# Gated cross-attention and mixture-of-experts blocks: queries turned on the TensorE between two groups of scores, one place sooner

## The reference, cut to what matters

```python
# x: (4, 512, 512) tokens; ctx_512: (4, 512, 128), keys and values at once
def _L0_xattn_ref(q, k, v):              # _L1_xattn_ref computes the same
    QH, KVH = (32, 8); D = E // QH       # D = 16
    G = QH // KVH                        # 4 query heads share a head of keys
    qh = q.reshape(b, s, KVH, G, D).transpose(0, 2, 3, 1, 4)
    kh = k.reshape(b, s, KVH, D).transpose(0, 2, 1, 3)
    vh = v.reshape(b, s, KVH, D).transpose(0, 2, 1, 3)
    scores = jnp.einsum('bkgsd,bktd->bkgst', qh, kh) * scale
    attn = jax.nn.softmax(scores, axis=-1) / DROPOUT
    out = jnp.einsum('bkgst,bktd->bkgsd', attn, vh)
    return out.transpose(0, 3, 1, 2, 4).reshape(b, s, E)

x = x + jnp.tanh(g_xattn[0]) * _L0_xattn_ref(_layernorm(x, axis=-1), ctx_512, ctx_512)
x = x + jnp.tanh(g_ffn[0]) * _L0_ffn_ref(_layernorm(x, axis=-1), ...)   # 8 experts, top 2, and a shared one
x = x + jnp.tanh(g_xattn[1]) * _L1_xattn_ref(_layernorm(x, axis=-1), ctx_512, ctx_512)
x = x + jnp.tanh(g_ffn[1]) * _L1_ffn_ref(_layernorm(x, axis=-1), ...)   # 32 experts, top 6, and a shared one
```

## Time and profile before

| | |
|---|---|
| time, median of 3 runs | 2155.77 us (2149.66 to 2156.09) |
| profiled execution | 2151.34 us, its span 2149.6 us |
| PE busy | 1973.5 us (92%) |
| DVE busy | 1325.7 us (62%) |
| ACT busy | 1105.8 us (51%) |
| POOL busy | 752.2 us (35%) |
| line 597, the takes of the maxima (DVE) | x1024, 644.8 us |
| line 491, the exps (ACT) | x512, 494.0 us |
| line 386, the products for the maxima (PE) | x1024, 407.6 us |
| line 403, the scores for the exps (PE) | x1024, 326.7 us |
| line 418, the products with values (PE) | x2048, 274.5 us |

### The profile page before, as it was taken

How to read it: one execution, slowest core, us unless ns; L and a number is a source line. 1 busy time by engine, 2 the same in 40 slices (tenths; PEclk the granted TensorE clock), 3 DMA queues, 4 the chain that set the end, 5 groups by cost and what they waited for, 6 DMA issues and landing times. The chain is left out here.

```text
span 2149.6 us, 40775 instructions
## 1 busy us (share of the span) xinstructions
PE 1973.5 (92%) x10072; PEld 1222.5 (57%) x10073; DVE 1325.7 (62%) x2547; ACT 1105.8 (51%) x1801; POOL 752.2 (35%) x912
## 2 busy tenths in 40 slices
PE   5999999979999999993999999988789999999997
PEld 2444444334667658882434444433557888888886
DVE  7888888732234325533888888856776455555553
ACT  2777777832112115541577777763113566666664
POOL 3122222112201005554122222221664555565564
PEclk9999999989999999996799999999999999999998
DMA  5322222150000128765422222213005888888886
GB/s 162 88 60 63 56 64 62 29 217 19 1 0 1 69 83 197 169 111 123 132 70 56 56 60 66 56 49 107 0 5 174 190 187 198 200 204 205 202 196 103
DMA packets 96018, 219.90 MB, mean 102 GB/s; under 512 B 16930, under 2 KB 20004, under 8 KB 95908
## 3 DMA queue, kind: packets, MB, share of 16 engines
q1 hardware_dynamic: 61540, 138.80, 22.3%
q0 software_dynamic: 33792, 79.71, 19.1%
q10 hardware_dynamic: 576, 0.00, 0.0%
HBM read 114.64 MB, written 56.63 MB: 80 GB/s over the span
## 5 line engine op out<-in xcount | busy, mean ns | idle before, releaser
L597 DVE TENSOR_REDUCE maxima<-ring_ps 128x1 f32<-128x512 f32 x1024 | 644.8, 681 | 116.2 <-PE ring_ps L386 115.9
L491 ACT ACTIVATE probs<-score_ps 128x1024 f32<-128x1024 f32 x512 | 494.0, 1020 | 47.7 <-PE score_ps L403 45.3
L386 PE MATMUL ring_ps<-k_turned,q_turned 64*128 64x512 f32 x1024 | 407.6, 477 | 32.1 <-DMA q_turned<-q_lo 13.3
L1091 PE MATMUL bank_f<-w_gu_parts_f,xg_T_f 128*128 x1800 | 368.1, 353 | 2.0 <-issue 2.0
L386 PEld LDWEIGHTS ring_ps<-k_turned,q_turned 64*128 64x128 f32 x1024 | 176.9, 192 | 326.1 <-DVE maxima L597 205.8
L1091 PEld LDWEIGHTS bank_f<-w_gu_parts_f,xg_T_f 128*128 128x128 f32 x1800 | 326.6, 190 | 30.2 <-issue 2.6
L403 PE MATMUL score_ps<-q_turned,k_turned 64*128 64x512 f32 x1024 | 326.7, 450 | 14.7 <-ACT probs L491 14.3
L418 PE MATMUL out_ps<-probs,v_ones 128*32 128x512 f32 x2048 | 274.5, 608 | 0.8 <-ACT probs L491 0.7
L1116 PE MATMUL bank_f<-w_dn_parts_f,hg_T_f 96*128 (+1 forms) x888 | 242.6, 409 | 2.5 <-DVE hg_T_f L1653 1.4
L916 POOL DMA_INDIRECT out_x<-y_tok_f,idx_out_f x111 | 176.7, 1592 | 137.4 <-ACT y_tok_f L1291 104.9
L900 POOL DMA_INDIRECT xg_f<-xh_rows_f,idx_in_f x156 | 158.1, 1014 | 186.3 <-DVE idx_in_f L1543 114.5
(11 more groups left out here) (211 smaller groups left out, 2252.2 us busy)
## 6 DMA issues: line engine op xcount, KB each, us to landing
w_gu_f<-in_L_w_gu SPq DMA_DIRECT2D x64, 384.0 KB
q_turned<-q_hi SPq DMA_DIRECT2D x128, 128.0 KB, 2.6
w_dn_f<-in_L_w_dn SPq DMA_DIRECT2D x32, 384.0 KB
k_turned<-k_hi SPq DMA_DIRECT2D x128, 64.0 KB, 2.1
q_turned<-no_max SPq DMA_DIRECT2D x64, 128.0 KB, 2.6
q_turned<-q_lo SPq DMA_DIRECT2D x64, 128.0 KB, 2.6
xh_rows_f<-xh_f SPq DMA_DIRECT2D x8, 1024.0 KB, 9.0
w_gu_f<-in_L_w_gu SPq DMA_DIRECT2D x16, 512.0 KB
```

The costliest lines, as they stand in the source:

```text
L386: pe.matmul(ring(k, "max", i), q_turned[rows, slot, h // 2, c * P:(c + 1) * P], k_turned[rows, slot, :], start=True, stop=True).then_inc(m ...
L491: act.activation(probs[:, c % 2, pair, :, :], score_ps[:, pair, :, :], ACT.Exp, scale=float(D) ** -0.5).then_inc(exped, 1)
L597: dve.tensor_reduce(maxima[:, par, col:col + 1], ring(k, "max", i), AX.X, ALU.max).then_inc(max_taken, 1)
L1091: mm = pe.matmul(bank[:, half, 0:2 * F], xg_T[:, half, x_part, d, :], w_gu_parts[:, bass.ds(par, 1), w_part, d, :].rearrange("p a f -> p ( ...
```

## The change

Two numbers change: `TURN_Q_AT` from 5 to 4, and `COPY_Q_AT` from 6 to 5.

```diff
-TURN_AT, TURN_Q_AT, INVERT_AT = 2, 5, 8
-COPY_OUT_AT, COPY_TURN_AT, COPY_Q_AT = 1, 3, 6
+TURN_AT, TURN_Q_AT, INVERT_AT = 2, 4, 8
+COPY_OUT_AT, COPY_TURN_AT, COPY_Q_AT = 1, 3, 5
```

## The result

| | before | after |
|---|---|---|
| median of 13 runs | 2154.42 us (2149.66 to 2160.61) | 2148.47 us (2143.82 to 2152.71) |
| ratio | | 0.9975, 95% interval 0.9965 to 0.9986 |
| ordinary odd step (k = 5 of batches 0 to 2 apart) | 12.72 us | 12.27 us |
| step k = 5, batches 0 to 2 | 12.86 us | 12.42 us |
| even step | 11.57 us | 11.57 us |

The time lies in the range and 3 us from the number forecast; the gain is 5.4 us by the ratio (its interval is 3.0 to 7.5 us) where 7.9 were forecast. The profiled execution of after is by chance the slowest of its 13 runs (2152.71 us), so spans of single executions say nothing here; steps do.

The account below looks back on a forecast made before the run. Short waits between TensorE and the two engines reading its PSUM set the step. 20 x 0.42 - 4 x 0.13 = 7.9 us off 2151.34 gives 2143.4, plus 2 for level: 2145.5 us; range 2136 to 2154.

Parts of the forecast that it names:

- ordinary odd step: Odd attention steps apart from first steps and k = 3: 20 turns, each step ending 0.42 us sooner.
- The split of the 1.15 us: Extra time of an odd step over an even one: 0.58 us of transposes, 0.56 us of waiting for ScalarE.
- the wait for take 9: Product 11 in the odd step now waits for VectorE's take 9, losing 0.38 us of TensorE.
- The rival in which the ring does not bite: Product 11 finds its bank free: 0.8 us gained per turn, 21 us in all, about 2132; chance 0.11.
- the one in which GpSimd holds up VectorE: Queries' cast and subtraction slow takes 10 to 13: 0.87 us lost per turn, 23 us, about 2176; chance 0.05.
- The rival in which the wait only changes its name: The ring's wait takes all that ScalarE gives back; time within 2 us of now, 2152; chance 0.14.
- steps k = 3: Odd steps with a `k_lo` piece before take 9: 0.13 us later in batches 1 and 2, 0 in batch 0.
- The first odd step: Batch 0, k 1, without exps or products with values: the gap moves with the transposes, change 0.
- The change of tiling mode: Half-array products to whole-array transposes and back: 0.32 us included; a further drain shows only above 0.38 us.
- 28 turns: Query turns in odd steps: 20 ordinary, 4 k = 3 of batches 1 and 2, 2 of batch 0, 2 first steps.
- what was called a measurable change: Differences under 0.3% (6.5 us) were held not to be told from no change in this kernel.

## Why the prediction was right, and where its size was off

- *What bounds the step.* The split of the 1.15 us (0.58 of transposes, 0.56 of waiting for ScalarE) was right: the new place takes the second away, and moving the copy alone makes the same wait longer. In its stead stands the wait for take 9; an odd step now takes 0.70 us more than an even one.
- *The ordinary odd step.* Forecast 12.30 us, with product 11 0.72 behind product 10; measured 12.27 and 0.70. The term that was least certain, the wait for take 9, is confirmed by the run that starts take 9 sooner. The rival in which the ring does not bite is refuted by the rows of after, and so is the one in which GpSimd holds up VectorE: takes 9 to 11, two of which have the cast and the subtraction beside them, take 1.91 us, and 1.91 us in step k = 5 of batch 3, where neither is there. The rival in which the wait only changes its name holds in the steps k = 3, as forecast, and in no ordinary step that turns queries.
- *Steps k = 3.* Forecast 0.13 us longer, measured 0.15 to 0.18; in batch 0 the scatter of the clock's rise covers it. The first odd step: no change, as forecast.
- *The change of tiling mode.* 0.32 us from product 9 to the transposes, as the row said; no further drain shows, but product 10 waits for take 8 anyway, and a few hundredths of a microsecond would be hidden there.
- *The term that was missed is in the count of the sum.* "28 turns" were counted, but the price of the new place is a price of the ring, and the ring has 32 places for queries in its steps. In four of them nothing is turned, and there the whole 0.70 us is lost: 2.8 us. With this term the sum is 7.9 - 2.8 = 5.1, with the 0.02 us by which each ordinary step was better 5.5; measured are 5.4 by the ratio. The 7.9 lie just outside the interval of 3.0 to 7.5 us.
- *Chances.* A gain of 5.4 us is 0.25%, just under what was called a measurable change; 13 runs of each put the interval clear of 1 all the same. By the sum over the steps, the count that was missed is what moved it below the line.
- *What the number itself confirms is little.* The forecast of 2145.5 us rests on a level of 2153.4 for the kernel before, chosen between two readings of 3 runs; 13 runs put it at 2154.42. So 1 us of the 3 us by which the forecast was off is the level and 2 the gain, by the medians. The range is 18 us wide and takes in the case without a change. It is the steps that bear the mechanism out.

## What to carry to other kernels

Where buffers are handed round in a fixed order, an entry costs by its neighbours' waits, also in the rounds in which nobody uses it: count the places, not the uses, and let unused ones go. Work put into a stall is hidden only as far as it does not lengthen that stall. Here product 11 came 0.71 us behind product 10 where 0.34 would have done, a wait of 0.37; 0.58 us of transposes went ahead of it, and their place in the ring made the products wait one take longer. And replay the list on one step's clock with its own rows: that gave the step's length to 0.03 us, while whole executions of the kernel before scatter by 11.

## What the runs showed of the hardware that was not expected

- Behind stalls of TensorE like that of 1.26 us, the granted clock went from 1.00 to 0.50 for 3.4 us in some of the steps with this stall and not in others; with stalls of 0.42 us no profile of before shows it between the step k = 3 of batch 0 and the end of the attention.
- In layer 1 the clock stays at its lower level for 29.0 to 29.8 us behind the first max product in five of the six profiles of before and after, and for 39.0 us in the sixth; in one of the five it falls again for 3.4 us right after. The same step of the same program text takes 14.90 to 17.70 us by that. What decides between these forms no run here shows.
